# Unread products in thirteen of TensorE's waits in a fused decoder kernel

## The reference

```
x = x + tanh(g_xattn[0]) * L0_xattn(layernorm(x), ctx)   # stage a: 16 heads of 32, q and k normed
x = x + tanh(g_ffn[0])   * L0_ffn(layernorm(x))          # stage b: 512 -> 2048 -> 512, 8 bit x, ternary w
x = x + tanh(g_xattn[1]) * L1_xattn(layernorm(x), ctx)   # stage c: 16 heads of 128
x = x + tanh(g_ffn[1])   * L1_ffn(layernorm(x))          # d: latent attention, causal, rope; e: experts
```

## Time and profile before

| | |
|---|---|
| median of 3 runs | 2255.32 us (2254.62 to 2255.53) |
| span of the profiled execution | 2257.6 us |
| TensorE busy | 2145.6 us (95%), 17918 products |
| TensorE weight loads busy | 1788.6 us (79%) |
| VectorE, ScalarE, GpSimd busy | 1307.3, 1078.4, 677.1 us |
| mean granted TensorE clock | 0.984 |

### The profile page before, as it was taken

How to read it: one execution, slowest core, us unless ns; L and a number is a source line. 1 busy time by engine, 2 the same in 40 slices (tenths; PEclk the granted TensorE clock), 3 DMA queues, 4 the chain that set the end, 5 groups by cost and what they waited for, 6 DMA issues and landing times. The chain is left out here.

```text
span 2257.6 us, 43111 instructions
## 1 busy us (share of the span) xinstructions
PE 2145.6 (95%) x17918; PEld 1788.6 (79%) x17918; DVE 1307.3 (58%) x2283; ACT 1078.4 (48%) x1887; POOL 677.1 (30%) x684
## 2 busy tenths in 40 slices
PE   6999998899999999999999999999799999899996
PEld 5666666444489999999999999999677877799995
DVE  7666776689854445444544444454555455767764
ACT  4676633478744444333433344333455554425553
POOL 4111210266512221111111111211255543125664
PEclk9999999999999999999999999999999999999998
DMA  7454202100032222321223123221000000258995
GB/s 261 160 170 134 81 11 113 57 1 1 29 131 108 89 100 106 112 75 64 86 94 113 64 87 119 79 70 49 25 2 2 2 2 30 85 187 262 275 274 103
DMA packets 46931, 215.30 MB, mean 95 GB/s; under 512 B 6161, under 2 KB 6161, under 8 KB 32401
## 3 DMA queue, kind: packets, MB, share of 16 engines
q1 hardware_dynamic: 29968, 139.13, 17.1%
q0 software_dynamic: 16768, 73.41, 11.3%
HBM read 169.00 MB, written 43.52 MB: 94 GB/s over the span
## 5 line engine op out<-in xcount | busy, mean ns | idle before, releaser
L336 POOL TENSOR_TENSOR c_prob<-c_prob,c_inv_mass 128x512 f32<-128x512 f32 x128 | 130.5, 1039 | 353.1 <-DVE c_inv_mass L328 353.1
L318 ACT ACTIVATE c_prob<-abc_banks,c_neg_peak 128x256 f32<-128x256 f32 x256 | 117.7, 472 | 178.0 <-DVE c_neg_peak L310 178.0
L50 PE MATMUL abc_banks<-c_ctx,c_wk_hi 128*128 128x256 f32 x512 | 146.6, 286 | 2.3 <-DVE c_qt_lo L2148 2.3
L50 PE MATMUL abc_banks<-bc_xt,bc_wq_hi 128*128 128x256 f32 x512 | 147.7, 288 | 0.0
L51 PE MATMUL abc_banks<-bc_xt,bc_wq_hi 128*128 128x256 f32 x512 | 144.9, 283 | 0.0
L52 PE MATMUL abc_banks<-bc_xt,bc_wq_lo 128*128 128x256 f32 x512 | 144.8, 283 | 0.0
L51 PE MATMUL abc_banks<-c_ctx,c_wk_hi 128*128 128x256 f32 x512 | 143.8, 281 | 0.0
L52 PE MATMUL abc_banks<-c_ctx,c_wk_lo 128*128 128x256 f32 x512 | 143.6, 281 | 0.0
L231 PE MATMUL abc_banks<-ab_wq,b_xqt 128*128 128x512 bf16 x512 | 117.2, 380 | 5.8 <-DVE b_h L202 3.7
L1898 POOL DMA_DIRECT2D c_ctx<-kept_scratch x24 | 13.2, 551 | 347.0 <-PE abc_banks L52 347.0
L3220 POOL DMA_INDIRECT out<-el_r,e_target x44 | 82.8, 1882 | 75.6 <-DMA out<-el_r,e_target 60.6
(11 more groups left out here) (564 smaller groups left out, 7192.4 us busy)
## 6 DMA issues: line engine op xcount, KB each, us to landing
x_res<-b_w SPq DMA_DIRECT2D x48, 512.0 KB, 4.7
bc_xt<-kept_scratch POOLq DMA_DIRECT2D x24, 1024.0 KB, 5.1
c_ctx<-kept_scratch POOLq DMA_DIRECT2D x24, 1024.0 KB, 5.1
e_raw<-e_w SPq DMA_DIRECT2D x15, 1536.0 KB, 9.2
bc_raw<-c_w SPq DMA_DIRECT2D x16, 1024.0 KB, 4.9
h_res<-e_w SPq DMA_DIRECT2D x7, 1536.0 KB, 9.6
kept_scratch<-bc_xt SPq DMA_DIRECT2D x8, 1024.0 KB, 3.9
kept_scratch<-c_ctx SPq DMA_DIRECT2D x8, 1024.0 KB, 3.9
```

Source lines behind the costliest of these rows:

```text
L50: pe.matmul(out, lhs[0], rhs[1], start=first, stop=False)
L318: ins = act.activation(self.prob[:, u % 2, j, :], self.s_ps[:, j, :], ACT.Exp, bias=self.neg_peak[:, u % 2, j:j + 1], accum_out=self.mass[ ...
L336: pool.tensor_tensor(part, part, self.inv_mass[:, u % 2, js].unsqueeze(2).to_broadcast([P, 2, SEQ]), ALU.mult).then_inc(self.prob_done, 1)
```

## The change

A helper issues `n` products of 128 x 128 by 128 x 512 into one bank. Each starts and ends its own accumulation, and nothing reads what they leave; the next real product into the bank overwrites it. Calls of it stand at thirteen places in TensorE's lists: five in stage a, four in c, four in d. Where the bank could still be in use, a wait for its last reader goes ahead. In stage d the claim of the bank of `turn_peaks` moves ahead of its wait for the maxima. The operands are weights that are on chip at that time.

```diff
--- before.py
+++ after.py
@@ -50,6 +50,13 @@
     pe.matmul(out, lhs[0], rhs[1], start=first, stop=False)
     pe.matmul(out, lhs[0], rhs[0], start=False, stop=False)
     return pe.matmul(out, lhs[1], rhs[0], start=False, stop=last)
+
+
+def keep_busy(pe, bank, w, of, n):
+
+
+    for _ in range(n):
+        pe.matmul(bank, w, of, start=True, stop=True)
 
 
 def wait_apart(eng, sem, value, begun):
@@ -807,6 +814,12 @@
                 pe.wait_ge(summed, PIECES)
                 return pe.matmul(bank[:, 0:PIECES], ones[:, :], part[:, :], start=True, stop=True)
 
+            def busy(name, s, w, n):
+
+                if use_of[name, s] >= BANKS:
+                    pe.wait_ge(free_of(name, s), use_of[name, s] // BANKS)
+                keep_busy(pe, bank_of(name, s), w_hi[w][:, 0, 0:P], w_hi[w][:, 0, :], n)
+
             pe.wait_ge(begun, 1)
             pe.wait_ge(blanked, 4)
             pe.wait_ge(spread_done, 1)
@@ -834,6 +847,9 @@
                     if i == 1:
                         use("mean", 0, mean)
                     queries(i + 1, 0)
+                if i == BATCH - 1:
+                    pe.wait_ge(o_raw_done, 2 * i)
+                    keep_busy(pe, o_ps[:, :, :].rearrange("p h q -> p (h q)"), w_hi[WO][:, 0, 0:P], w_hi[WO][:, 0, :], 7)
                 if now:
                     turned_scores(i, 1)
                     weigh(i, 0)
@@ -868,6 +884,8 @@
                     early.turn_x(pe, 0, x_turned)
                 if nxt:
                     scores(i + 1, 0)
+                if i == BATCH - 2:
+                    busy("n1", i, WO, 9)
                 if here(i + 2):
                     keys(i + 2, 0)
                 if nxt:
@@ -881,12 +899,18 @@
                     keys(i + 2, 1)
                 if nxt:
                     scores(i + 1, 2)
+                if i == -1:
+                    busy("mt", 0, WK, 8)
+                if i == BATCH - 2:
+                    busy("o0", i, WO, 5)
                 if now:
                     if i == 0:
                         pe.wait_ge(w_lo_done[WO], 1)
                     outputs(i, 0)
                 if nxt:
                     scores(i + 1, 3)
+                if i == -1:
+                    busy("mt", 0, WK, 8)
                 if now:
                     outputs(i, 1)
             early.up(pe, 0, 1)
@@ -2008,6 +2032,11 @@
                     return mm
                 use("dl", LAST, emit)
 
+            def busy(n):
+
+                pe.wait_ge(att.o_lo_done, LAST)
+                keep_busy(pe, att.o_ps[:, 0, :], w_hi[WO][:, 0, 0:P], w_hi[WO][:, 0, :], n)
+
             for s in TURNS:
                 now, nxt = here(s), here(s + 1)
                 if now:
@@ -2026,6 +2055,7 @@
                 if s == LAST:
                     turn_rows(0)
                     turn_rows(1)
+                    busy(6)
                 if now:
                     att.turn(pe, s, 1)
                 if nxt:
@@ -2034,6 +2064,7 @@
                 if turned(s + 2):
                     turn_x(s + 2, 0)
                 if s == LAST:
+                    busy(5)
                     latents()
                 if now:
                     weigh(s)
@@ -2042,7 +2073,10 @@
                 if nxt:
                     values(s + 1, 0)
                     values(s + 1, 1)
+            pe.wait_ge(ring_free[use_of["o0", LAST] % 2], use_of["o0", LAST] // 2)
+            keep_busy(pe, bank_of("o0", LAST), w_hi[WO][:, 0, 0:P], w_hi[WO][:, 0, :], 7)
             outputs(LAST)
+            keep_busy(pe, att.o_ps[:, 0, :], w_hi[WO][:, 0, 0:P], w_hi[WO][:, 0, :], 4)
 
         @block.scalar
         def _(act):
@@ -2559,8 +2593,12 @@
                 turn(f"kt{t}", s, heads(kf, t))
 
             def turn_peaks(i):
+                bank = claim("mt", i)
+                if i == 0:
+                    keep_busy(pe, bank, parts["v_u"][0][:, 0:P], parts["v_u"][0], 7)
+                if i == BATCH - 1:
+                    keep_busy(pe, bank, halves[0][0][:, 0, 0:P], halves[0][0][:, 0, :], 7)
                 pe.wait_ge(peak_done, C * i + C)
-                bank = claim("mt", i)
                 for t in range(TB):
                     mm = pe.transpose(bank[:, t * P:(t + 1) * P], neg_peak[:, t, :], ident[:, :])
                 mm.then_inc(ring_ready, 1)
@@ -2664,6 +2702,9 @@
                 if nxt:
                     queries(i + 1, 1)
                     keys(i + 1, 0)
+                if i == BATCH - 1:
+                    pe.wait_ge(o_raw_done, 2 * i)
+                    keep_busy(pe, o_ps[:, :, :].rearrange("p h q -> p (h q)"), halves[0][0][:, 0, 0:P], halves[0][0][:, 0, :], 5)
                 if now:
                     turned_scores(i, 1)
                     weigh(i, 0)
@@ -2720,6 +2761,7 @@
                     latents("lk", 1)
                 if nxt:
                     scores(i + 1, 3)
+            keep_busy(pe, s_ps[:, 0, :], halves[0][0][:, 0, 0:P], halves[0][0][:, 0, :], 4)
 
         @block.scalar
         def _(act):
```

## The result

The changed kernel takes 2248.73 us (median of 7 runs, 2245.84 to 2256.7) against 2255.32 for the kernel before in the same session (7 runs, 2252.53 to 2263.93). The ratio is 0.9968, 95% interval 0.9956 to 0.9981: faster by 6.6 us. The prediction said 2244.1 with a range of 2240.0 to 2250.8. The profiled execution spans 2245.8 us, where 2246.4 was forecast for a span "like this one". (The time of an execution is 1.7 us more than its span in nearly all runs; here 2247.51.)

The account below looks back on a forecast made before the run. TensorE, 95% busy, was taken as the bound, losing time to half clock behind waits. Gains of 13.5 us less 2.3 for new falls, 11.2 off the 2255.32 median, gave 2244.1 us, range 2240.0 to 2250.8.

Parts of the forecast that it names:

- The treated waits keep the clock: Stages a, c and d: waits filled with products keep TensorE at full clock behind them, giving back 13.5 us in sum.
- The fillers are free under their cover: Filler blocks before existing waits end 0.2 to 1.0 us before what TensorE waits for, so cost nothing.
- The four at the end of c: Four fillers behind stage c's last output product delay the stage barrier, costing 0.2 us (0 to 0.4).
- The rival of outlasting fillers: Blocks starting at low clock take 0.427 us a product and outlast their waits: 8.8 to 9.6 us, 2265; chance 0.04.
- New falls, 2.3 us booked: Untreated waits, redrawn as work runs earlier, newly lose the clock: 2.3 us booked, between 0 and 4.5.
- 1924 (`d_inv_mass`): Untreated 2.3 us wait in stage d that kept the clock; a new fall behind it would cost some 0.7 us.
- 631: Untreated 2.3 us wait for `c_qt_lo` that kept the clock; a new fall there would cost about 1.5 us.
- 443: Untreated 2.2 us wait for `b_h` that kept the clock; a new fall there would cost some 0.7 us.
- the same 11.2 gives 2244.1 us: Whole kernel: the net 11.2 us expected off the 2257.6 us profiled span is also taken off the 2255.32 median.
- The falls move: Rival: redrawn waits and one or two treated ones lose the clock, 5 to 7 us go, 2247 to 2250.5; chance 0.25.
- the forecast: Main case for the whole kernel: 9 to 14 us off, chance 0.63.
- What is gained is waited for: Rival: fillers don't hold the clock or the gain is waited for, so 2255, within 0.2%; chance 0.08.

Follow-up runs that it names:

- e7: Changed kernel plus one GpSimd wait: in stage a's first turn its subtraction waits until VectorE has scaled a_qf; 2243.79 us, ratio 0.994.
- e5: Changed kernel with all thirteen filler counts doubled; 2259.62 us, ratio 1.001 to the kernel before.
- e10: e7 plus fillers at six untreated waits, less the four fillers behind stage d's last output product; 2241.18 us, ratio 0.9931.
- e2: The changed kernel, unchanged, measured once more; 2249.84 us, ratio 0.9954 to the kernel before.
- e1: The kernel before, unchanged, measured once more; 2257.35 us, ratio 0.9997.
- e4: Changed kernel with only the eight filler blocks of stages c and d, those of stage a set to 0; 2253.63 us, ratio 0.9976.
- e6: Changed kernel with all filler counts halved, rounded down; 2248.09 us, ratio 0.9955 to the kernel before.
- e8: e7 plus fillers meant for six untreated waits, some of stage a's blocks placed a turn early; 2246.81 us, ratio 0.9954.
- e11: The kernel before, without fillers, plus the one GpSimd wait of e7; 2256.83 us, ratio 0.9998.
- e3: Changed kernel with only the five filler blocks of stage a, the counts in c and d set to 0; 2250.69 us, ratio 0.9976.

## Why the prediction was right, and where it was off

- **The treated waits keep the clock: right.** By column: start of a 3.4 (3.2 said); turns 6 and 7 3.7 (3.2); end of c and start of d 4.0 (5.55, of which 1.8 went into the new fall at 1617; e7, without it, has 5.8); last turn of d 1.1 (1.6). Sum 12.2, or 14 without the fall, against 13.5.
- **The fillers are free under their cover: right** (idle time is left behind all thirteen, e5 loses what sticks out). The four at the end of c cost 0.1 us (0.2 said), by the start of VectorE's first instruction behind the barrier; for those in d no cost was measured (e10). The rival of outlasting fillers is what e5 is.
- **New falls, 2.3 us booked: near in size, partly in place.** 1924 (`d_inv_mass`) fell and cost 1.2 in after and e2, not 0.7; 631 fell in e2 and cost 1.6 (1.5 said); 443 fell in e1, e2 and e10 and cost next to nothing (e10, where it fell alone, has +0.2 in that column). With the 1.8 at 1617 the new falls cost 3.0 in after and 4.6 in e2. The fall at 1933.53 of before is gone in after, but stands some 5 us later in e4, e5, e6 and e8 in spite of the four. Not foreseen: 1.0 to 1.3 at the start of e, and the start of a at 36, which is no untreated wait of the earlier trace rows but VectorE held up by GpSimd (3.0).
- **The step that was mis-sized: "The median of the runs is 2255.32, 2.3 below that span; the same 11.2 gives 2244.1 us".** In spans the gain was 11.8, in medians 6.6 (0.32%), and 0.46% in e2. That the span came within 0.6 us of its forecast is luck: beside the 12.2 of the treated columns, 5.3 us were lost that the sum did not foresee (31 to 42, and to 1960), and 5.0 were gained in stretches without fillers (ahead of 31, to 215, the end).
- **Why the medians gained less.** The 2.3 set a time against a span. Like with like, the profiled execution of before, with a span of 2257.6, took some 2259.3 and was 4.0 above its median, and the one of after, 2247.51, was 1.2 below its own: 11.8 - 4.0 - 1.2 = 6.6. What the profiled execution of before had more than the median one is shown only in part. It was not the share of low clock (see e1). At the treated places e1 lost 1.8 less (-1.0 -1.2 +0.3 +0.1) and e11 0.9 less. The loss up to 1960 (+2.3, +2.6) is in nearly every kernel with fillers in d, and in none without. By one execution each, 12.2 - 1.8 - 2.3 = 8.1. The columns that are drawn anew (31-42, to 215, to 640, the end) moved by up to 5, 5, 1.6 and 10 us between executions and take part in each median; how the rest down to 6.6, 1.5 us, splits among them is not shown.
- **The rivals.** The measured 2248.73 lies where "The falls move" put it (2247 to 2250.5, chance 0.25), not 9 to 14 us off as the forecast had it (0.63); the range held because it spans both. Of that rival's mechanism one half came true: falls at untreated waits cost more than was booked. The other half did not: none of the nine treated places ahead of stage e lost the clock in six profiles with the full counts. "What is gained is waited for" is wrong for a to d (e3); in stage e it happened in some executions (e10, e11) and not in others (e7).

## What to carry to other kernels

Here waits of 1.6 to 3 us on the busiest engine cost up to as much again behind them, in work at half pace; products nobody reads give it back for nothing if they end before what is waited for, and cost themselves to the last one if not, so take count and place from the trace of the very turn. Before a sum is taken off a median, look at a second profile of the same program: terms that are not in both are draws, and a span is to be compared with spans, not with times. And when a gain does not show at the end, look in the last stage for a second chain.

## What the hardware showed beside this

- Whether an instruction of 2.4 us on GpSimd begins 0.27 us (after) or 0.51 us (e5) behind a pair of VectorE's decides over 2.1 us of VectorE, and with the fall behind it 3.0 to 5.2 us of the kernel.
- At 202 us TensorE's wait was 3.9 to 4.0 us and not 2.7 in e2, e5 and e8, where ScalarE stood 1.1 us in its queue for a load of weight pieces ahead of the rounding that TensorE needed. Whether it does is not settled by how early ScalarE is: its instruction ahead of that wait began at 190.14 in e2, and at 190.23 in e10, where no such wait came.
- The end behind the last product, 16.2 us in after and 21.0 in e11 (span less the start of the last product), depends on when the last adding stores land, by up to 5 us.
